# Transposing the quantised hidden activations with DMA transfers instead of TensorE

## The reference

```
def _quant_act(x):
    scale = 127.0 / clip(max(abs(x), axis=-1), 1e-5)
    return clip(round(x * scale), -128, 127) / scale
def _bitlinear(x, w):
    return einsum('bsi,oi->bso', _quant_act(x), _quant_weight(w))   # ternary weights
h = gelu(_bitlinear(x, w1))        # 256 -> 1024
x = x_res + _bitlinear(h, w2)      # 1024 -> 256
```

## Time and profile before

| | us |
|---|---|
| median of 3 runs | 289.79 (288.65 to 290.27) |
| the profiled execution, its own time | 289.39 |
| its span, first to last instruction | 287.6 |
| PE / DVE / ACT / POOL busy | 256.9 / 165.7 / 145.2 / 129.9 |

### The profile page before, as it was taken

How to read it: one execution, slowest core, us unless ns; L and a number is a source line. 1 busy time by engine, 2 the same in 40 slices (tenths; PEclk the granted TensorE clock), 3 DMA queues, 4 the chain that set the end, 5 groups by cost and what they waited for, 6 DMA issues and landing times.

```text
span 287.6 us, 6503 instructions
## 1 busy us (share of the span) xinstructions
PE 256.9 (89%) x2554; PEld 198.3 (69%) x2554; DVE 165.7 (58%) x435; ACT 145.2 (51%) x269; POOL 129.9 (45%) x133
## 2 busy tenths in 40 slices
PE   8976559799999797999999999999989898999653
PEld 8953437576677475777777777777768787888532
DVE  3467455865552344256665555555555779889840
ACT  1331513443444677355555666555543266888662
POOL 1332000531021666098896968585895024332330
PEclk9999759999999899799999999999999999999996
DMA  7999999950094101001010010100000000000011
GB/s 227 341 390 396 236 395 390 394 204 2 1 334 142 36 0 39 2 1 39 0 37 5 2 38 2 39 2 0 2 2 2 0 2 1 22 18 21 19 35 38
DMA packets 18477, 27.74 MB, mean 96 GB/s; under 512 B 1424, under 2 KB 11792, under 8 KB 18448
## 3 DMA queue, kind: packets, MB, share of 16 engines
q1 hardware_dynamic: 17008, 26.35, 27.1%
q10 hardware_dynamic: 1440, 0.99, 1.1%
HBM read 26.28 MB, written 1.05 MB: 95 GB/s over the span
## 4 chain that ended last, share of the span: by engine, by line
PE 70%; SPq 9%; DVE 7%; DMA 4%; ACT 4%; issue 4%; POOL 1%; POOLq 0%; DVEq 0%; ACTq 0%
PE b L1103 15%; PE b L910 12%; PE b L911 10%; PE b L912 10%; PE b L1128 6%; PE b L1116 6%; DMA cT<-in_ctxT 4%; SPq L171 3%; SPq L262 2%; PE b L1000 2%; PE b L981 2%; PE b L1219 2%; PE b L1158 1%; SPq L258 1%; DVE qsc L881 1%
## 5 line engine op out<-in xcount | busy, mean ns | idle before, releaser
L531 ACT ACTIVATE phi<-b 128x512 f32<-128x512 f32 x64 | 34.8, 596 | 45.7 <-PE b L1103 45.7
L351 POOL TENSOR_TENSOR sq_lo<-sq,sq_hi 128x512 fp32r<-128x512 f32 x32 | 40.8, 1284 | 28.8 <-ACT sq_hi L475 28.2
L741 DVE CAST x_hi<-b 128x512 fp32r<-128x512 f32 x32 | 22.1, 692 | 53.4 <-ACT sq_hi L475 53.4
L307 POOL TENSOR_TENSOR lnr<-lnv,mh 128x1 f32<-128x1 f32 x16 | 8.7, 546 | 56.1 <-DVE lnv L624 56.1
L910 PE MATMUL b<-nT_lo,wp_hi 128*128 128x512 f32 x64 | 27.2, 424 | 0.0
L474 ACT ACTIVATE sq<-b 128x512 f32<-128x512 f32 x32 | 19.2, 599 | 13.9 <-PE b L912 13.8
L911 PE MATMUL b<-nT_hi,wp_lo 128*128 128x512 f32 x64 | 25.5, 398 | 0.0
L912 PE MATMUL b<-nT_hi,wp_hi 128*128 128x512 f32 x64 | 25.3, 395 | 0.0
L743 DVE TENSOR_TENSOR x_lo<-b,x_hi 128x512 fp32r<-128x512 f32 x32 | 22.1, 691 | 1.1
L1116 PEld LDWEIGHTS b<-phi,phi 128*64 128x64 f32 x512 | 16.2, 138 | 7.7 <-issue 5.1
L910 PE MATMUL b<-wo_lo,yT_hi 128*128 128x256 f32 x64 | 18.6, 290 | 2.4 <-DVE yT_lo L845 2.4
(11 more groups left out here) (145 smaller groups left out, 643.8 us busy)
## 6 DMA issues: line engine op xcount, KB each, us to landing
cT<-in_ctxT SPq DMA_DIRECT2D x8, 1028.0 KB, 13.1
cn<-in_ctx SPq DMA_DIRECT2D x8, 1024.0 KB, 14.6
wv_raw<-in_aWv SPq DMA_DIRECT2D x1, 1024.0 KB, 18.8
wp_raw<-in_aWq SPq DMA_DIRECT2D x8, 128.0 KB, 2.2
wp_raw<-in_aWk SPq DMA_DIRECT2D x8, 128.0 KB, 2.3
w_raw<-in_w1T SPq DMA_DIRECT2D x1, 1024.0 KB, 4.9
w_raw<-in_w2T SPq DMA_DIRECT2D x1, 1024.0 KB, 7.7
wo<-in_aWo SPq DMA_DIRECT2D x1, 1024.0 KB, 10.2
```

The source lines that it names most:

```text
L351: nc.gpsimd.tensor_tensor(sq_lo[s % 2][t][:], sq[s % 2][t][:], sq_hi[s % 2][t][:].bitcast(F32), ALU.subtract).then_inc(sq_l, 1)
L531: nc.scalar.activation(phi[s % 2][t][a][:], (b2, b3)[a][:], ACT.Exp).then_inc(f_exp, 1)
L741: nc.vector.tensor_copy(x_hi[s % 2][t][:], proj_bank(s, t)).then_inc(x_h, 1)
```

## The change

For each group SP issues eight transposing transfers from `hq` to `hqT`, both in SBUF, one for each 128x128 block. SP waits for `hq_r` (cast_h(g) is done) and for `f2_mm` (layer2(g-1) is done with `hqT`) before the first of them. Each adds 16 to a new semaphore `hqT_dma` when it has landed; `layer2(g)` waits for all eight of group g, and `cast_h(g)` for all eight of group g-1. TensorE no longer runs `hqTt`, ScalarE no longer runs `hqTc`. The store of group g-1 stands in SP's program behind the eight transfers of group g.

```
-            for g in range(NG):
-                sp.wait_ge(fin_r, g + 1)
-                sp.dma_start(outv[g], fin[g % 2][:]).then_inc(stored[g % 2], 16)
+            for g in range(NG + 1):
+                if g < NG:
+                    sp.wait_ge(hq_r, g + 1)
+                    if g >= 1:
+                        sp.wait_ge(f2_mm, g)
+                    for c in range(HC):
+                        sp.dma_start(hqT[:, c, :], hq[:, c * P:(c + 1) * P], transpose=True).then_inc(hqT_dma, 16)
+                if g >= 1:
+                    sp.wait_ge(fin_r, g)
+                    sp.dma_start(outv[g - 1], fin[(g - 1) % 2][:]).then_inc(stored[(g - 1) % 2], 16)
...
             def cast_h(g):
                 act.wait_ge(hr_r, g + 1)
                 if g >= 1:
-                    act.wait_ge(hqT_mm, g)
+                    act.wait_ge(hqT_dma, 16 * HC * g)
...
-                if 0 <= i - 3 < NG:
-                    hqTc(i - 3)
...
             def layer2(g):
-                pe.wait_ge(hqT_cp, g + 1)
+                pe.wait_ge(hqT_dma, 16 * HC * (g + 1))
...
-                if 0 <= i - 3 < NG:
-                    hqTt(i - 3)
```

More of the change, by code:

```diff
@@ L227, in build @@
             sem(n) for n in ("h_mm", "h_act", "h_scale", "hr_r", "hq_r", "hqT_mm", "hqT_cp", "f2_mm", "fin_r"))
+        hqT_dma = sem("hqT_dma")
         block = stack.enter_context(nc.Block())
```

## The result

| | median us | runs |
|---|---|---|
| before | 289.14 | 5 (288.41 to 290.27) |
| after | 349.71 | 5 (349.45 to 351.3) |

The ratio is 1.211, 95% interval 1.206 to 1.216: 60.6 us slower. The prediction said 335 us, from 293 to 410. The profiled execution after took 351.3 us with a span of 349.5; it is the slowest of the five.

The account below looks back on a forecast made before the run. TensorE's work was taken to bound the last stage's turns, and one group's latencies its end. 247.08 + 8T + 7d, with T = 9.1 and d = 2.1, gave 334.6 us, forecast as 335, range 293 to 410.

Parts of the forecast that it names:

- The loop p = T + d: Last stage, per group: landing, then cast or layer2, then the next group's issue; p = 11.2 us.
- T: Time from SP's first issue of a group to the landing of its eighth transfer; forecast 9.1 us.
- The formula: Whole kernel time after the change: 247.08 + 8T + 7d, giving 334.6 us.
- d = 2.1 at half clock, 1.2 at full: After each landing, the longer of cast and layer2 with hops between engines; 2.1 us chosen for a long T.
- serial: Rival for SP's transfers: each runs only after its predecessor, T = 13.6 or more; above 371 us, chance 0.24 with slower cases.
- The pipelined rival: SP's transfers pipeline like ordinary ones: T = 4.6, d = 1.2, 292.3 us; chance 0.20 for 291 to 313 us.
- The hidden rival: Transfers hide in TensorE's 5.7 us turn if T stays below 4.24; not slower than before, chance 0.09.
- The work removed: TensorE loses 0.45 us in each full turn of the last stage, 2.2 us over five turns.
- The store at nothing: The store behind eight issues on SP costs nothing; without that cover, the eight issues' time once a group.
- Contention at nothing: The transfers' 256 KB a group beside a DMA system 1 to 10% busy in the last stage, priced at nothing.

Follow-up runs that it names:

- D: The changed kernel with two hq and two hqT, the loop's waits moved one group back, still eight transfers a group; 334.37 us, ratio to before 1.155.
- B: The changed kernel with sixteen transposing transfers a group, each 64 source rows by 128 columns, in place of eight; 431.09 us, one run.
- F: The changed kernel with matmuls nobody reads ahead of layer2, 44 in most turns, to keep TensorE busy; 351.71 us, ratio to before 1.214.
- G: The changed kernel with fewer, larger filler matmuls ahead of layer2, 22 of 512 columns a turn, 46 in the last two; 347.64 us, ratio 1.205.
- C: The changed kernel with one transposing transfer of 128 by 1,024 a group in place of eight of 128 by 128; 289.1 us, one run.
- A: The changed kernel with eight plain copies from hq to hqT in place of the transposing transfers, blocks left untransposed; 309.01 us, one run.
- E: The kernel before, plus four transposing transfers a group on SP to a tile nobody reads; 297.76 us, ratio 1.026.
- I: The kernel before with 16 and 8 filler matmuls ahead of the last group's hqTt and layer2; 289.57 us, ratio 0.9996.
- L: The changed kernel with one transfer a group, two hq and hqT, and filler matmuls ahead of the last aqTt and last two layer2; 287.96 us, ratio to before 0.9954.

## Why the prediction was right, and what was mis-sized

The direction, the mechanism and the range held. Point by point:

- **The loop p = T + d** was right. p was 13.17 us with T = 11.15 and d = 2.02, and D, which opened it, came out at 334 where 333 was expected.
- **The formula** held to 1 us: with T = 11.15 and d = 2.02 it gives 247.08 + 89.2 + 14.1 = 350.4 us, and the profiled execution took 351.3. The 0.9 us are in the chain: the first cast ended at 241.20 and not at 240.52, and T was 11.27 us in the first group and 11.39 in the fourth (280.84 to 292.23). B was called at 432 and took 431.
- **d = 2.1 at half clock, 1.2 at full**: measured 2.0 (after), and 1.2 in F and G. In after it was the half clock that counted, as the prediction chose. The clock fell as the thinly filled stretches had shown, and further, to 0.50 in the last three turns.
- **T was mis-sized**, 9.1 us where 11.15 was measured; eight times the difference is 16.4 us, of which d gives 0.6 back, and that makes the 15 us between 335 and 349.7. Both parts of it were low: 1.06 us from issue to issue was 1.27, and a landing of 1.7 was 2.3 to 2.4. The 0.41 us that stood for small transfers is the spacing of two loads of 1,024 KB. I had chosen the middle between pipelined and serial. The truth was neither: transfers overlap, and SP's own issuing sets the pace. The trace of before had no row of it, so that the middle of two wrong mechanisms came within 0.21 us of the spacing is luck.
- **The figure of the Trainium skill** (VectorE: DVE Perf Modes, "The three transpose paths", 1,309 ns for 128x128) gave 349 us by the formula, nearer than my own choice, and the spacing of 1.27 us agrees with it. But it is no price by size: B and C have 1.23 and 1.24 us for half and for eight times the block.
- **The pipelined rival** was wrong in its price: A shows 0.64 us for plain copies, so T = 4.6 was not to be had with eight transfers at all. The Trainium skill's rule that transposing DMAs are as fast as regular ones (Advanced Engine Details and Errata, "X-Bar Transpose (TRN2)") does not hold for the issue, 1.23 against 0.60 us; for the landing it nearly does, 2.3 against 1.8.
- **The hidden rival** came true in another kernel: with one transfer T = 3.1, below the 4.24 at which I had put the turn, and C took 289.1 where the hidden case gives 289.39 - 2.2 + (3.1 - 1.73) = 288.6. Two errors cancel in that: the turns gave more than 2.2 (the last cast is 2.55 us earlier), and the last group lost 2.11 and not 1.37, because its transfer waited 0.8 us for layer2 of the group before, which the case did not have.
- **The work removed**, 0.45 us a turn from TensorE, was there in C, as 0.56 (5.57 against 6.13), and hidden in after behind the wait.
- **The store at nothing** was right in after. Without its cover, in D, it cost its own 0.58 us a group and not the eight issues' time. **Contention at nothing** holds within 0.3 us (E, at about the same rate of transfers as after).

## What to carry to other kernels

Price a DMA in a chain by the issues of its queue first, and count them: eight transposing transfers cost eight times 1.27 us of SP, one of eight times the size costs it once. If a transfer replaces an engine's operation between single buffers, write down the loop that its landing closes (T + d a turn, compared with the turn as it is) before asking what the engine gains. Filler matmuls for the clock shortened the turns where they reached almost to the work whose clock they were to keep (G, 12.32 us instead of 13.17), and gained nothing where they began at half clock and held up the work behind them (I) or ended 2.5 us early (the last layer2 of L).

## What the runs showed of the hardware that I had not expected

- A transposing transfer occupied SP for 1.23 us whether it moved 64x128, 128x128 or 128x1024 elements of two bytes (B, after, C), and landed after 2.3 us or, for the largest, 3.1.
- A plain copy between two places in SBUF occupied SP for 0.60 us and landed after 1.8 (A), against 0.33 to 0.37 us for an issue to or from HBM on a queue with nothing under way. The store after the transposing transfers took 0.58 (after).
- TensorE's clock: in after it was at half all through the turns with 1.9 to 4.2 us of work in 13, and at 0.76 with 7.5. The last layer2 ran at half clock 2.5 us after 14 filler matmuls that had run at full (L).
- Single transposing issues took 1.6 to 2.6 us in D to G and L, and none of after's 64 exceeded 1.25. A 16 KB packet of the instruction queue was under way during each of them. Whether it is the cause is open.
